# Local pass of a graph network: first and last layer multiplied in full 32-bit words, the eight middle layers in three rounded parts

## The reference

```
def conv(x, W, b):                  # agg over the edges, then the node itself
    h = x @ W
    return segment_sum(h[src] * norm, dst) + (dinv * dinv)[:, None] * h + b
x = l2norm(conv(x, W1, b1))                           # 128 -> 256, "first"
f = lambda z: conv(l2norm(conv(z, Wf1, bf1)), Wf2, bf2) + z   # "mid", "end"
k1 = f(x); k2 = f(x + 0.5 * k1); k3 = f(x + 0.5 * k2); k4 = f(x + k3)
x = x + (k1 + 2 * k2 + 2 * k3 + k4) / 6
x = conv(x, W2, b2)                                   # 256 -> 128, "last"
x = layernorm(x_in + x)
```

## Time and profile before

| | |
|---|---|
| median of 3 runs | 7417.72 us (7416.8 to 7420.82) |
| the profiled execution | 7411.88 us |
| its span | 7408.9 us |
| local pass in it | about 253 to 2481 us |

### The profile page before, as it was taken

How to read it: one execution, slowest core, us unless ns; L and a number is a source line. 1 busy time by engine, 2 the same in 40 slices (tenths; PEclk the granted TensorE clock), 3 DMA queues, 4 the chain that set the end, 5 groups by cost and what they waited for, 6 DMA issues and landing times. The chain is left out here.

```text
span 7408.9 us, 157945 instructions
## 1 busy us (share of the span) xinstructions
PE 6235.8 (84%) x37260; PEld 5136.6 (69%) x37260; DVE 6278.8 (85%) x16996; ACT 3963.8 (54%) x11296; POOL 4124.5 (56%) x4269
## 2 busy tenths in 40 slices
PE   7698998888999657989989998999888766987776
PEld 3688888888888535867776677667756554865664
DVE  8788888888888777879878987998799887878887
ACT  6566777777777576733671157115722233764443
POOL 0454444447600476855776677667744465646665
PEclk8799999999999898999999999999999998989998
DMA  0465555554444466879779977997799865543432
GB/s 2 118 167 161 158 161 160 162 161 154 144 145 140 149 188 196 247 253 301 230 225 319 336 235 225 326 336 232 226 372 388 283 186 157 170 145 121 125 124 83
DMA packets 981282, 1483.86 MB, mean 200 GB/s; under 512 B 156967, under 2 KB 450705, under 8 KB 980647
## 3 DMA queue, kind: packets, MB, share of 16 engines
q1 hardware_dynamic: 685479, 922.39, 37.4%
q0 software_dynamic: 141504, 309.42, 16.3%
q10 hardware_dynamic: 153664, 244.12, 9.1%
HBM read 902.58 MB, written 573.11 MB: 199 GB/s over the span
## 5 line engine op out<-in xcount | busy, mean ns | idle before, releaser
L1346 PE MATMUL bank<-c_rows,sums_all 128*128 128x256 f32 (+1 forms) x3920 | 1321.7, 420 | 534.9 <-DVE c_rows L1497 377.3
L751 PE MATMUL bank<-wf_w,c_xt 128*128 128x256 f32 x6272 | 1614.5, 380 | 1.9 <-DVE y L1555 1.9
L1391 ACT ACTIVATE c_xt<-bank 128x512 f32<-128x512 f32 (+1 forms) x980 | 556.2, 568 | 1579.4 <-PE bank L1357 1575.5
L1346 PEld LDWEIGHTS bank<-c_rows,sums_all 128*128 128x128 f32 x3920 | 634.5, 194 | 966.5 <-DVE c_rows L1497 787.3
L1317 POOL DMA_INDIRECT c_rows<-t_tab,src_pair x784 | 869.1, 1109 | 709.0 <-PE bank L1346 552.3
L751 PEld LDWEIGHTS bank<-wf_w,c_xt 128*128 128x128 f32 x6272 | 1133.4, 191 | 126.9 <-ACT c_xt L1391 3.4
L1497 DVE SCALAR_TENSOR_TENSOR c_rows<-bank,carry,c_rows 32x256 f32<-32x256 f32 (+1 forms) x1950 | 913.9, 469 | 265.7 <-PE bank L1346 166.1
L1317 POOL DMA_INDIRECT c_rows<-z_tab,src_pair x784 | 764.8, 975 | 288.8 <-issue 186.9
L741 PE MATMUL bank<-wf_hi,lx_hi 128*128 128x256 f32 x3200 | 713.4, 305 | 98.8 <-ACT lx_hi L1017 59.6
L1017 ACT ACTIVATE lx_hi<-bank 128x512 fp32r<-128x512 f32 (+1 forms) x1000 | 574.1, 574 | 392.2 <-PE bank L986 385.6
L1511 DVE SCALAR_TENSOR_TENSOR c_u<-bank,lead,c_own 128x256 f32<-128x256 f32 x1764 | 758.5, 467 | 0.5
(11 more groups left out here) (334 smaller groups left out, 14447.0 us busy)
## 6 DMA issues: line engine op xcount, KB each, us to landing
c_z<-z_tab SPq DMA_DIRECT2D x882, 256.0 KB
z_tab<-lz SPq DMA_DIRECT2D x400, 256.0 KB, 3.1
t_tab<-lt SPq DMA_DIRECT2D x400, 256.0 KB
z_tab<-y ACTq DMA_DIRECT2D x392, 256.0 KB
c_own<-z_tab SPq DMA_DIRECT2D x392, 256.0 KB
t_tab<-y ACTq DMA_DIRECT2D x392, 256.0 KB
c_own<-t_tab SPq DMA_DIRECT2D x392, 256.0 KB
fl_x<-x_tab SPq DMA_DIRECT2D x396, 128.0 KB
```

Source lines behind the costliest of these rows:

```text
L751: last = nc.tensor.matmul(out, x(k), w[:, k, :], start=(k == 0), stop=(k == ks - 1 and not bias))
L1346: nc.tensor.matmul(psum[s % 2][:, i * win:(i + 1) * win], sums[:, j * 2 + i, :], rows[:, s, i, 0:win], start=True, stop=True).then_inc(S[" ...
L1391: nc.scalar.activation(xt[:, s % 2].rearrange("p k n -> p (k n)")[:, 0:n], psum[2 + s % 2][:, 0:n], ACT.Copy).then_inc(S["copied"], 1)
```

## The change

The first and the last layer use `full_product` on the 32-bit words. Their input is copied out of PSUM by the same ACT instruction, into new tiles `x_first` and `x_last` of type float32, two buffers each, in place of `x_hi`. DVE's `low` is left out for these slots, and PE's wait for it. Three waits change with it: a transpose that re-uses a bank waits for `high` of the slot four back where that slot has no `low`; `high` waits for the product two back in the first and the last block (four back elsewhere, as before); and the weights of these two layers are no longer split.

```diff
 def split_weights(nc, a, S, m):
-    parts = [("w1", ...), ("wf1", ...), ("wf2", ...), ("w2", ...)]
+    parts = [("w1", ...), ("w2", ...), ("wf1", ...), ("wf2", ...)]
...
-                for n, (name, ks, width, _) in enumerate(parts):
+                for n, (name, ks, width, _) in enumerate(parts[2:]):
...
+        x_first = sb("lx_first", [P, 2, 1, H2])
+        x_last = sb("lx_last", [P, 2, 2, H2])
...
+        parted = [1 if kind[layer[q]] in ("mid", "end") else 0 for q in range(Q)]
-            "turned": one, "high": one, "low": one, "product": one, "taken": one,
+            "turned": one, "high": one, "low": parted, "product": one, "taken": one,
...
+        def full_rows(b, q):
+            return (x_first if layer[q] == 0 else x_last)[:, q // 2 % 2]
...
                 def turn(b, q, odd):
-                    if prev:
+                    if prev and parted[prev[1]]:
                         pe.wait_ge(S["low"], ph.at("low", *prev))
+                    elif prev:
+                        pe.wait_ge(S["high"], ph.at("high", *prev))
...
                 def multiply(b, q, odd):
                     pe.wait_ge(S["high"], ph.at("high", b, q))
-                    pe.wait_ge(S["low"], ph.at("low", b, q))
+                    if parted[q]:
+                        pe.wait_ge(S["low"], ph.at("low", b, q))
...
+                        if not parted[q]:
+                            last = full_product(nc, psum[4 + n][:, i * width:(i + 1) * width],
+                                                lambda k: full_rows(b, q)[:, k, i * P:(i + 1) * P],
+                                                m[w + "_w"], ks)
+                            continue
...
                 def high(b, q, odd):
-                    prev = ph.back(b, q, 4)
+                    alone = isinstance(b, int) and b in (0, blocks) and not parted[q]
+                    prev = ph.back(b, q, 2 if alone else 4)
...
                 def low(b, q, odd):
+                    if not parted[q]:
+                        return
```

More of the change, by code:

```diff
@@ L266, in gnn_kernel @@
         early("dst_f", [P, TE])
-        for name, ks, width in (("w1", 1, H2), ("wf1", 2, H2), ("wf2", 2, H2), ("w2", 2, D)):
+        for name, ks, width in (("wf1", 2, H2), ("wf2", 2, H2)):
             early(name + "_hi", [P, ks, width], F32R)
@@ L687, in split_weights @@
 def split_weights(nc, a, S, m):
-    parts = [("w1", 1, H2, "L0_gnn_W1"), ("wf1", 2, H2, "L0_gnn_Wf1"), ("wf2", 2, H2, "L0_gnn_Wf2"),
-             ("w2", 2, D, "L0_gnn_W2")]
+    parts = [("w1", 1, H2, "L0_gnn_W1"), ("w2", 2, D, "L0_gnn_W2"), ("wf1", 2, H2, "L0_gnn_Wf1"), ("wf2", 2, H2, "L0_gnn_Wf2")]
     with nc.sbuf_tensor("b_rest", [P, H2], F32) as b_rest, nc.sbuf_tensor("not_one", [P, 1], F32) as not_one:
@@ L1013, in high @@
                     act.wait_ge(S["turned"], ph.at("turned", b, q))
-                    prev = ph.back(b, q, 4)
+                    alone = isinstance(b, int) and b in (0, blocks) and not parted[q]
+                    prev = ph.back(b, q, 2 if alone else 4)
                     if prev:
                         act.wait_ge(S["product"], ph.at("product", *prev))
-                    nc.scalar.activation(x_hi[:, k].rearrange("p k n -> p (k n)")[:, 0:n], psum[k][:, 0:n],
-                                         ACT.Copy).then_inc(S["high"], 1)
+                    nc.scalar.activation((x_hi[:, k] if parted[q] else full_rows(b, q)).rearrange("p k n -> p (k n)")[:, 0:n],
+                                         psum[k][:, 0:n], ACT.Copy).then_inc(S["high"], 1)
                 def begin_rest(b, q, odd):
@@ L1081, in low @@
                 def low(b, q, odd):
-                    n = H2 if layer[q] == 0 else 2 * H2
+                    if not parted[q]:
+                        return
+                    n = 2 * H2
                     k = bank(b, q)
```

## The result

| | before | after |
|---|---|---|
| median | 7417.68 us (4 runs) | 7336.55 us (4 runs, 7332.18 to 7338.54) |
| the profiled execution, its span | 7411.88, 7408.9 | 7338.54, 7336.8 |
| ratio | | 0.9889, 95% interval 0.9872 to 0.9906 |

The account below looks back on a forecast made before the run. In the local pass the bound was taken to go round DVE, ACT and PE. The terms 59.0 + 15.8 + 7.9 + 0.75 + 0.4 + 0.7 = 84.6 us, taken from 7417.7, gave 7333 us, range 7308 to 7385.

Parts of the forecast that it names:

- The bound goes round: Local pass, one block: DVE, then ACT, then PE sets the pace; a removed step counts only in its engine's stretch.
- `low` of the last layer, 59.0 us: DVE's stretch, slots 33, 35, 37, 39: 100 steps removed at 0.59 us each, 59.0 us gained.
- `low` of the first layer, 15.8 + 7.9: First-layer slots: removed steps of pace 0.33 us gain 15.8 us in slots 0 and 2, 7.9 in slot 4, nothing in slot 6.
- The part of slots 0 and 2: DVE's stretch, ahead of the first layer's first `take`: two steps of 0.33 us in 24 blocks, 15.8 us gained.
- The part of slot 4: DVE ahead of the `invert` that ACT awaits 0.40 us: wait shortened by 0.33 in 24 blocks, 7.9 us gained.
- PE's products, 0: First and last products on PE: 0.72 to 0.52 us and 1.38 to 0.61, in DVE's or ACT's stretches, so 0 gained.
- two rivals: Local pass: PE sets the pace, 7321 us, chance 0.05; or full products take four passes, 7488 us, chance 0.01.
- PE's waits ahead of end products: Sign in DVE's stretch: these waits, 0.71 and 1.51 us before, would get longer, growing by less than 0.6.
- The ends: Late `take` steps in the last block 0.75 us, first chain at the start 0.4, splitting of weights 0.7, all gained.
- The clock: Rival: PE's clock falls in DVE's stretch; for part of it 7376 us, chance 0.12; throughout 7600 us, chance 0.04.
- Another queue: Rival: POOL's tables or SP's stores set a block's pace, so no difference, 7418 us, chance 0.05.
- After the pass: Stages behind the local pass: the same instructions, so no difference expected.

Follow-up runs that it names:

- dead step: The changed kernel plus one DVE step of 128x512 that nobody reads, in one first-layer slot: in slot 4 7352.60 us, in slot 6 7335.71 us.
- dead `low`: The changed kernel with DVE's `low` of the first and last layer put back as work that nobody reads, products still in full words: 7409.25 us.
- first layer only: The changed kernel with the last layer back in three parts, with its `low` and split weights, so only the first layer in full words: 7385.42 us.

## Why the prediction was right, point by point

**The bound goes round, and only steps in an engine's own stretch count.** Right, and shown: the same dead step costs 13.8 us in slot 4 and nothing in slot 6, the product's shape alone is worth nothing, and ACT's and PE's stretches kept their lengths (28.27 and 16.19 us, as above).

**`low` of the last layer, 59.0 us.** The pair of slots shown above went from 5.36 to 4.74 us, 0.62 where 0.59 was forecast; alone, the layer gave 51.3 in 23 blocks, where the sum had 54.3. The sum left out that `take` would then start later behind `add_rest`, by some 0.1 us a slot (last section).

**`low` of the first layer, 15.8 + 7.9.** Right in both parts. The part of slots 0 and 2: DVE's list from the `take` of slot 37 to the first `take` of the first layer, which holds these two steps, went from 7.88 to 7.30 us (medians of 23 blocks), 0.58 where 0.66 was forecast. The part of slot 4: ACT's wait fell by 0.33 on average, and by 9.4 - 1.9 = 7.5 us in all, where 7.9 was forecast; with the first layer alone in full words it is 2.0. That layer alone gave 26.6 us in 23 blocks, where the sum had 22.8.

**PE's products, 0.** Right in its effect, wrong in its sizes; this is the step of the working that failed. The text read the records of the earlier trace rows as matmuls: "four matmuls of 128x256 in 1.03 us", so 0.26 each, about two passes. They are two matmuls (one tile, two halves of the input). A first product grew from 0.72 to 0.87, where 0.52 was forecast; a last one takes 0.89, not 0.61, which was the time of two matmuls and not of four. The rule of the Trainium skill ("FP8 and Floating Point Precision", TensorE Precision Notes) that true FP32 takes four passes was set aside on that reading. The trace agrees with it for 128x256: 0.43 against 0.12 for a rounded one, 3.6 times. At 128x128 it is 0.22 against 0.12, not quite twice a rounded one. So two rivals had wrong prices. Had PE set the pace, the gain would have been 100 x 0.49 - 100 x 0.15 = 34 us, about 7384, and neither 7321 nor 7488. None of this reached the time, because PE's waits covered it. It also made one sign come out wrong: PE's waits ahead of end products became shorter (0.71 to 0.41, 1.51 to 1.27), not longer.

**The ends.** DVE's two late `take` steps at the end of the pass are on time, in the changed kernel:

```profile
2389.88 0.42 DVE L1151 TENSOR_TENSOR lx<-bank,lrest 128x256 f32<-128x256 f32 x1
...
2392.42 0.42 DVE L1151 TENSOR_TENSOR lx<-bank,lrest 128x256 f32<-128x256 f32 x1
```

The splitting of weights lost its two steps: the starts of DVE's first and last step there lie 2.77 us apart and not 3.44, for 0.7 forecast. The 0.4 us at the start were not there: from the first `high` to the first `square` it is 5.21 us, and was 5.19, since each `high` waits for a transpose of gathered input some 2.4 us after the last.

**The clock.** One sign came out wrong here. PE idles less, not more (busy 1452.96 of 1600 us from 600 to 2200, and 1436.70 before). Yet the granted clock isn't 1.00 outside the turns: it fell in DVE's stretch in six of the loop's ten blocks without a turn, and before the change in two of the ten. The prediction had read one block where it didn't. The changed kernel from 976 to 982 us, with PE's rows:

```profile
976.00:982.00 6.00, 6.00 (x35) 5.62 (x36) 5.44 (x20) 3.09 (x12) 2.72 (x3) 0.72 0.42 143
...
975.85 0.51 PE L740 MATMUL bank<-wf_hi,lx_hi 128*128 128x256 f32 x2 [1.81 <-DVE lx_lo L1101]
...
977.17 0.63 PE L740 MATMUL bank<-wf_lo,lx_hi 128*128 128x256 f32 x2
977.60 0.63 PE L740 MATMUL bank<-wf_hi,lx_lo 128*128 128x256 f32 x2
...
978.45 1.78 PE L750 MATMUL bank<-w_w,lx_first 128*128 128x256 f32 x4
980.06 0.60 PE L993 MATMUL bank<-ident,lz 128*128 128x128 f32 x4
```

PE had stood for 1.81 us; then two matmuls took 0.43 us, the lower level of 1.2 GHz, and the first product 1.61 in place of 0.87. The prediction had named such a fall as a sign that it is wrong. The price that the rival put on it didn't come, though: the six blocks took 84.2 us (median) and the other four 84.2. The kernel without `low` and with three products, whose clock fell in none of these blocks, took 84.2 too.

**Another queue.** Not seen: the blocks shrank by what DVE lost. The turn of the loop itself moved, which the sum had left out; DVE and PE there, to be held against the earlier trace rows:

```profile
1231.61 0.42 DVE L1124 TENSOR_TENSOR lrest<-lx_add,b 128x256 f32<-128x256 f32 x1 [4.02 <-issue]
...
1228.84 0.44 PE L993 MATMUL bank<-ident,lx_in 128*128 128x128 f32 x2 [4.07 <-issue]
```

At this turn DVE stands 4.02 us and not 4.67, PE 4.07 and not 3.02; over nine turns DVE stood 3.53 us on average, and 4.05 before. Blocks with a turn won 3.7 us, blocks without one 3.1. That they meet the 3.35 of the sum together is in part luck: the blocks without a turn, for which the sum was made, fell short of it, and the turns, which it left out, made up for that. What ends this wait wasn't tried.

**After the pass** nothing was forecast to change. The rest of the profiled execution is 10.8 us longer after (4947.1 against 4936.3 us); with the same instructions there, the other runs have 4937.5 to 4947.8, so single executions scatter by as much. The pass alone, to the start of its last `high`, is 82.9 us shorter (2472.6 to 2389.7).

## What to carry to other kernels

Where the bound goes round between engines, ask of each step in whose stretch it lies: the same 0.6 us was worth 14 us in one slot and nothing two slots later. Then trade in that stretch alone: full-word products of 128x256 cost PE more than three rounded ones, pay where PE waits for DVE (layers 0, 4, 5 and 9: 7278 us), and give next to nothing when put everywhere (7329 us). Before a matmul is priced from rows, hold the count of rows against the matmuls in the code. And read a wait over all blocks before it is called typical: one block showed 0.21 us where the mean was 0.07, and a clock of 1.00 that six other blocks didn't have.

## What the runs showed of the hardware that was not expected

- A full-word matmul leaves two records. It takes 0.22 us at 128x128 (0.89 for four) and 0.43 at 128x256; a rounded one takes 0.12 at either size (1.38 for twelve at 128x128 in the earlier trace rows). Against three rounded parts the full one therefore wins at 128 columns and loses at 256.
- DVE's `take` of the last layer now starts 0.61 us after `add_rest`, whose result it reads (1138.42 to 1139.03); before it was 0.51 (1173.13 to 1173.64 on the same two steps). It goes with the missing `low` and not with the product: the median over all slots is 0.51 in every run that has a `low` right ahead of `add_rest` (before, dead `low`, first layer only) and 0.60 in every run that has none there, the one with three parts included. Why the two stand further apart then isn't shown. Four times a block, this takes back some 0.3 us of the 3.35.
